# Routing and experts of layers 2 and 3 in one stage, with batched scores, a scan for the slot numbers and a table built from stationary one-hots

## The chip, the cores and the metric

The kernel runs on one core of one Trainium2 chip. The metric is the device time of one launch in microseconds (us). The engines are TensorE (PE: matmuls, and its weight loads, PEld), VectorE (DVE), ScalarE (ACT), GpSimd (POOL) and SyncE (SP, which here issues most DMA transfers). They run their own instruction streams and meet only at semaphores. L1666 is line 1666 of the kernel's source; `x4` behind a row is a count.

## The reference

A decoder of four layers works on x, 16 sequences of 112 tokens of 256 numbers, all in 32-bit floating point. Each layer adds a gated cross-attention and then a gated feed-forward part. In layers 2 and 3 the latter is a mixture of experts, of which each token uses its best two:

```python
# layer 2: 8 experts with 1024 hidden units, biases, RMS norm
xn = x * rsqrt(mean(x * x) + eps) * ln_w
vals, idx = top_k(xn @ Wg + bg, 2)
w = softmax(vals)
out = sum over the two experts e of w_e * ((silu(xn @ W1a[e] + b1a[e]) * (xn @ W1b[e] + b1b[e])) @ W2[e] + b2[e])
# layer 3: 9 experts with 704 hidden units
s, idx = top_k(sigmoid(x @ gate.T + bias), 2)
s = s / (sum(s) + 1e-20)
out = sum over the two experts e of s_e * ((silu(x @ w1[e].T) * (x @ w3[e].T)) @ w2[e].T)
# both: x = x + tanh(g_ffn) * out, where the part's own input is layernorm(x)
```

## The kernel before

The program is a list of stages in `flamingo`: attention and feed-forward for each layer. A stage is one `nc.Block()`, with one function for each engine, and all engines meet at its end. In layers 2 and 3 the feed-forward part is two such stages, `route_stage` and `experts_stage`.

`route_stage` (L1568) has 16 blocks of 112 tokens, with tokens on the partitions. DVE gathers mean and variance from `row_stats` (L164), POOL takes the root as a power (L109; in layer 2 twice, since the RMS factor follows from the first), and DVE writes the normed rows `r_kept` (L1832). SP stores each block to `p_rows` in device memory (L1666). For each block PE transposes two pieces (L1698), ACT copies them to `r_xT` (L1773, L1776), PE multiplies them, as stationary operand, with the gate weights (L1707) and adds the bias with a matmul of ones (L1714), and DVE copies 8 or 9 logits (L1845).

After all 16 blocks DVE finds the best two of each token (L1870, L1891) and writes them as one-hots, `r_chosen` (L1896). Each chosen pair of token and expert gets a slot; slots are numbered by expert, and each expert's slots are rounded up to whole tiles of 128. To number them, PE sums the one-hots over the tokens above and over all tokens (L1746), DVE sums over the 32 columns by doubling (L1922, L1923), turns the totals into tiles per expert and the expert of each tile, `p_expert` (L1940), and then into a slot per pair (L1942 to L1951). Then it writes which tile (`r_in_tile`, L1953 to L1958, once with the token's number and once with its share) and which place in the tile (`r_at_slot`, L1961) each pair has. PE multiplies the two (L1752, 32 matmuls with the 128 places as stationary operand and 70 or 72 columns): its result, the table, holds for each place and tile the token and its share. DVE turns it into `p_take`, `p_put` and `p_part` (L1967 to L1970). The stage ends.

`experts_stage` (L2070) runs over T tiles of 128 slots, 35 in layer 2 and 36 in layer 3. SP reads a tile's expert and loads that expert's weights (L2177, L2183, L2188), two tiles ahead: 1 MB each for w1, w3 and w2 in layer 2, some 2.2 MB in all in layer 3. POOL gathers the tile's rows (`e_x_in`, L2149), PE transposes them (L2215), ACT copies them to `e_xT` (L2257, L2260). PE then makes the hidden units chunk by chunk (L2226), ACT and DVE apply silu and product (L2270, L2297, L2302), PE multiplies with w2 (L2237), DVE scales (L2311, L2315), and POOL adds the rows to `p_sums` (L2160), which ACT's queue has filled with x at the stage's start (L2281). SP loads x back from the sums at the end (L2202).

Constants and weights of a later stage are noted with `core.request` and issued by SP where a stage calls `core.load_requested` (L119): in `experts_stage` behind tile 1, for the attention of layer 3. The attention weights lie in `attention_room`, those of layer 1's experts in `net_room`. The order on each engine is the order of the code.

## Time and profile before

| | |
|---|---|
| median of 3 runs | 2956.69 us (2954.8 to 2957.62) |
| profiled execution, its own time | 2955.2 us |
| its span, first to last instruction | 2953.2 us |
| granted TensorE clock, mean over the span | 0.942 |
| PE, PEld, DVE, ACT, POOL busy | 92%, 70%, 52%, 44%, 21% |
| routing and first expert matmul, layer 2 | 1735.08 to 1822.49 |
| routing and first expert matmul, layer 3 | 2561.90 to 2646.02 |

The time in the table's second line lies 2.0 us above the span, which is what is around it. A row of the timeline gives start and duration in us, engine, line, operation, tiles, count, and in brackets how long the engine was idle before and what it waited for. In the table of stretches the busy times stand in the order PE, PEld, DVE, ACT, POOL, with the number of rows, and the clock is a share of full speed, 1.00 for 2.4 GHz and 0.50 for 1.2 GHz. A 32-bit matmul leaves two rows, a transpose one.

### The profile page before, as it was taken

What the parts mean: (1) busy time and instruction counts of PE and PEld (TensorE: products, weight loads), DVE (VectorE), ACT (ScalarE), POOL (GpSimd) and SP (SyncE); (2) the same over time, 40 slices, a digit from 0 to 9 for tenths busy, and PEclk for the clock granted to TensorE, in tenths of its full rate; (3) what the DMA queues carried; (4) which work ended last, traced back from release to release, by engine and by line L of the source; (5) the groups of instructions that cost most, each with busy time, mean ns of one, the idle gap of its engine ahead of it and who ended that gap; (6) DMA issues with size and microseconds to landing.
All of it is one profiled execution on the core that took longest, in us unless ns stands there. A gap on an engine that the chain in (4) does not pass through costs nothing. (4 is left out here: it accounts for less than half of the span.)

```text
span 2953.2 us, 57870 instructions
## 1 busy us (share of the span) xinstructions
PE 2705.3 (92%) x20048; PEld 2068.7 (70%) x20048; DVE 1546.3 (52%) x4193; ACT 1297.9 (44%) x3605; POOL 616.9 (21%) x562
## 2 busy tenths in 40 slices
PE   6999978999999999698999975999988999859998
PEld 4777755666666666555666665999986777648887
DVE  4776666555555555345777743333326777532222
ACT  4777732433434434212766641333336777402222
POOL 1656550000000000001444410222220000003332
PEclk9999989999999999589999976999999999759999
DMA  3000010000000000010000005999971000039897
GB/s 118 17 17 17 12 69 8 13 7 13 13 7 13 12 7 1 29 32 8 17 23 17 17 26 187 337 327 331 325 242 31 22 18 23 19 111 308 307 308 239
DMA packets 92438, 269.24 MB, mean 91 GB/s; under 512 B 25672, under 2 KB 51528, under 8 KB 77864
## 3 DMA queue, kind: packets, MB, share of 16 engines
q1 hardware_dynamic: 74984, 244.21, 23.9%
q0 software_dynamic: 13632, 18.62, 2.9%
q10 hardware_dynamic: 3616, 3.67, 0.4%
q8 instruction: 128, 2.10, 0.3%
q14 instruction: 78, 0.64, 0.1%
HBM read 249.82 MB, written 18.48 MB: 91 GB/s over the span
## 5 line engine op out<-in xcount | busy, mean ns | idle before, releaser
L755 PEld LDWEIGHTS a_full_ps<-ident,a_probs 112*125 112x125 f32 x2688 | 368.0, 190 | 130.1 <-issue 63.6
L2226 PEld LDWEIGHTS e_ab_ps<-e_xT,e_w 128*128 128x128 f32 x3824 | 439.1, 193 | 20.2 <-issue 12.2
L2226 PE MATMUL e_ab_ps<-e_xT,e_w 128*128 128x128 f32 x3824 | 446.6, 277 | 5.5 <-DMA e_w<-in_L2f_w 2.3
L755 PE MATMUL a_full_ps<-ident,a_probs 112*125 112x112 f32 x2688 | 418.3, 281 | 18.7 <-DVE a_pT L1111 5.8
L862 ACT ACTIVATE a_probs<-a_masked,a_negmax 112x375 f32<-112x375 f32 x512 | 305.5, 599 | 280.3 <-DVE a_negmax L1085 280.2
L1111 DVE COPY a_pT<-a_full_ps 125x448 f32<-125x448 f32 x448 | 276.5, 621 | 254.0 <-PE a_full_ps L755 250.8
L656 PE MATMUL a_full_ps<-attention_room 128*125 128x256 f32 (+1 forms) x960 | 330.1, 472 | 10.9 <-ACT a_qT L854 3.3
L648 PE MATMUL a_full_ps<-attention_room 128*128 128x375 f32 x896 | 324.1, 490 | 1.4 <-ACT a_q_raw L850 0.7
L1085 DVE CUSTOM_DVE_ANT_0 a_masked<-a_sc_ps,a_mask_add 112x375 f32<-112x375 f32 x512 | 249.7, 544 | 29.9 <-PE a_sc_ps L742 29.9
L773 PEld LDWEIGHTS a_o_ps<-a_pT,a_v 125*32 125x32 f32 (+1 forms) x5376 | 164.0, 118 | 134.8 <-issue 106.7
L862 ACT ACTIVATE a_probs<-a_sc_ps,a_negmax 112x375 f32<-112x375 f32 x384 | 216.6, 576 | 91.1 <-DVE a_negmax L1091 91.0
L742 PE MATMUL a_sc_ps<-a_kT,a_qT 32*112 32x375 f32 (+1 forms) x1792 | 241.9, 514 | 5.1 <-ACT a_probs L862 3.1
L2237 PE MATMUL e_y_ps<-e_w,e_hid 128*128 128x256 f32 x992 | 232.9, 383 | 0.0
L656 PEld LDWEIGHTS a_full_ps<-attention_room 128*125 128x125 f32 x960 | 166.5, 189 | 92.4 <-issue 65.7
L773 PE MATMUL a_o_ps<-a_pT,a_v 125*32 125x112 f32 (+1 forms) x5376 | 216.0, 265 | 14.4 <-DVE a_pT L1111 10.8
L1091 DVE TENSOR_REDUCE a_negmax<-a_sc_ps 112x2 f32<-112x750 f32 x192 | 171.3, 934 | 95.0 <-PE a_sc_ps L742 95.0
L2160 POOL DMA_INDIRECT p_sums<-e_y_out,p_put x71 | 112.6, 1586 | 486.1 <-DVE e_y_out L2311 288.4
L648 PEld LDWEIGHTS a_full_ps<-attention_room 128*128 128x128 f32 x896 | 160.4, 194 | 71.3 <-issue 4.0
L2270 ACT ACTIVATE e_silu<-e_ab_ps,e_b 128x128 f32<-128x128 f32 x280 | 102.3, 367 | 242.4 <-PE e_ab_ps L2226 223.8
L2237 PEld LDWEIGHTS e_y_ps<-e_w,e_hid 128*128 128x128 f32 x992 | 179.9, 190 | 32.0 <-issue 11.9
L525 POOL TENSOR_TENSOR a_rstd<-a_rstd,minus_half 112x1 f32<-112x1 f32 x64 | 35.1, 549 | 781.4 <-DVE a_rstd L1008 774.3
L2297 DVE SCALAR_TENSOR_TENSOR e_hid<-e_ab_ps,e_b,e_silu 128x128 f32<-128x128 f32 x280 | 97.8, 351 | 172.1 <-ACT e_silu L2270 135.4
(251 smaller groups left out, 3629.3 us busy)
## 6 DMA issues: line engine op xcount, KB each, us to landing
e_w<-in_L2f_w SPq DMA_DIRECT2D x105, 1024.0 KB, 6.7
e_w<-in_L3f_w SPq DMA_DIRECT2D x72, 768.0 KB, 5.5
attention_room<-in_ctxT SPq DMA_DIRECT2D x64, 375.0 KB, 3.1
e_w<-in_L3f_w SPq DMA_DIRECT2D x36, 640.0 KB
e_b<-in_L2f_b SPq DMA_DIRECT2D x35, 128.0 KB, 7.8
p_rows<-r_kept SPq DMA_DIRECT2D x32, 112.0 KB, 1.8
p_sums<-x_all ACTq DMA_DIRECT2D x2, 1792.0 KB, 18.3
attention_room<-in_L0x_spline_wT SPq DMA_DIRECT2D x1, 2048.0 KB, 10.4
```

The source lines that it names most:

```text
L648: mm = pe.matmul(use_ps[:, 0:SK], wk[:, c, u[1] * P:(u[1] + 1) * P], ctxT[:, par, c, :], start=(c == 0), stop=(c == DC - 1))
L656: mm = pe.matmul(use_ps[0:KT, 0:v_width], ctxT[:, par, c, k * KT:(k + 1) * KT], wv[:, c, part * v_width:(part + 1) * v_width], start=(c == ...
L742: pe.matmul(sc_ps[:, a, 0:SK], lhs, kT[r:r + k, par, c, :], start=True, stop=True)\
L755: mm = pe.transpose(full_ps[0:KT, bank_of["turn", i, k], (j % 4) * S:(j % 4 + 1) * S], probs[:, i % 2, a, t * KT:(t + 1) * KT], ident[0:S, ...
L773: mm = pe.matmul(o_ps[a % WIDE * VW:(a % WIDE + 1) * VW, block * S:(block + 1) * S], v[:, par, t, head(i, a), :], pT[:, i % 2, KC * a + t, :],
L862: act.activation(probs[:, i % 2, a, 0:SK], src, ACT.Exp, bias=negmax[:, m:m + 1], scale=-1.0 if mask else 1.0, accum_out=rowsum[:, par, n: ...
L1085: dve.tensor_tensor_reduce(out=masked[:, i % 2, a, :], in0=sc_ps[:, a, 0:SK], in1=bias, scale=-1.0, scalar=FLT_MAX, op0=ALU.add, op1=ALU.m ...
L1091: dve.tensor_reduce(negmax[:, m:m + 2], sc_ps[:, 2 * a:2 * a + 2, 0:SK], AX.X, ALU.max, negate=True).then_inc(s_max.sem, 1)
L1111: dve.tensor_copy(pT[:, i % 2, 4 * k:4 * (k + 1), :], full_ps[0:KT, bank_of["turn", i, k], 0:4 * S] .rearrange("p (j s) -> p j s", j=4)).t ...
L2160: pool.indirect_dma_start(plan.sums, bass.IndirectOffsetOnAxis(plan.put[:, t:t + 1], 0), y_out[:, t % 2, :], None, compute_op=ALU.add).the ...
L2226: mm = pe.matmul(ab_ps[:, (par * FC + f) % RING, i * SLOTS:(i + 1) * SLOTS], w[:, par, c, f * P:(f + 1) * P], xT[:, c, :], start=(c == 0), ...
L2237: mm = pe.matmul(y_ps[:, par, 0:D], hid[parts[f], f, :], w2[parts[f], par, f, :], start=(f == 0), stop=(f == FC - 1))
```

## The change

One function, `moe_stage`, takes the place of both stages. What it does otherwise:

- Norm: three parts of 2, 6 and 8 blocks, one power each; in layer 2 the RMS factor is worked into the same power.
- Scores: blocks go in pairs, four pairs in flight in four PSUM banks. ACT copies a pair (448 numbers a partition). The gate weights, padded to 32 columns, are the stationary operand; four pairs are scored into the four quarters of a bank. The result is copied, turned back with two transposes, and DVE adds the bias. Best two and one-hots are made for each half of 8 blocks. In layer 2 DVE scales the gate weights by `ln_w`.
- Slots: one scan numbers a token's pairs by expert; PE sums only its last column, 8 or 9 columns. A second scan takes the place of the product with `before`.
- The expert list is finished ahead of the shares; SP waits for it alone (`s_expert`) and then loads weights.
- One-hots: four groups of 8 columns. DVE writes `spots`, the token part and the places; POOL multiplies `spots` by the share. PE takes 99 or 100 columns as stationary operand and 128 places as moving columns, group by group, then two transposes turn the table's rows and shares.
- Rooms: `in_tile`, `spots` and `xT` lie in `attention_room`, `at_slot` in `net_room`. So the loads for attention in layer 3 move behind tile 34.
- POOL clears semaphores after the norm. ACT's copy of x to the sums is its first instruction. PE has no instruction in its waits for the one-hots and for the first rows.

PE in layer 2, from the last scores to the first expert matmul. Before (`r_table_ps` is the table, `e_x_ps` the first tile's rows, `e_ab_ps` its hidden units):

```order
L1707 MATMUL r_l_ps<-route_room,r_xT 112x8 x2
L1714 MATMUL r_l_ps<-route_room,ones 112x8
L1707 MATMUL r_l_ps<-route_room,r_xT 112x8 x2
L1714 MATMUL r_l_ps<-route_room,ones 112x8
L1746 MATMUL r_count_ps<-r_chosen,route_room 112x256
L1746 MATMUL r_count_ps<-r_chosen,r_every_one 112x256
L1752 MATMUL r_table_ps<-r_in_tile,r_at_slot 128x70 x32
L1659 UNCONDITIONAL_BRANCH
L2208 UNCONDITIONAL_BRANCH
L2215 MATMUL e_x_ps<-ident,e_x_in 128x128 x2
L2226 MATMUL e_ab_ps<-e_xT,e_w 128x128 x32
```

The change (all results are in `m_banks`; 32x224 are scores of four pairs, 99x128 is the table):

```order
L2294 MATMUL m_banks<-ident,m_kept 128x112 x20
L2303 MATMUL m_banks<-attention_room,route_room 32x224 x8
L2294 MATMUL m_banks<-ident,m_kept 128x112 x4
L2310 MATMUL m_banks<-ident,m_logitsT 112x128 x2
L2294 MATMUL m_banks<-ident,m_kept 128x112 x8
L2303 MATMUL m_banks<-attention_room,route_room 32x224 x8
L2310 MATMUL m_banks<-ident,m_logitsT 112x128 x2
L2330 MATMUL m_banks<-m_order,route_room 112x8
L2330 MATMUL m_banks<-m_order,m_every_one 112x8
L2337 MATMUL m_banks<-net_room,attention_room 99x128 x32
L2342 MATMUL m_banks<-ident,m_table 128x35 x2
L2350 MATMUL m_banks<-ident,m_x_in 128x128 x2
```

The scores come in two lots of eight, the count has 8 columns, the table 128, and no block ends between table and first tile.

DVE in layer 2, from the count to the number of tiles of each expert. Before:

```order
L1919 COPY r_total_a<-r_count_ps 112x256
L1922 COPY r_total_b<-r_total_a 112x8
L1923 TENSOR_TENSOR r_total_b<-r_total_a 112x248
L1922 COPY r_total_a<-r_total_b 112x16
L1923 TENSOR_TENSOR r_total_a<-r_total_b 112x240
L1922 COPY r_total_b<-r_total_a 112x32
L1923 TENSOR_TENSOR r_total_b<-r_total_a 112x224
L1922 COPY r_total_a<-r_total_b 112x64
L1923 TENSOR_TENSOR r_total_a<-r_total_b 112x192
L1922 COPY r_total_b<-r_total_a 112x128
L1923 TENSOR_TENSOR r_total_b<-r_total_a 112x128
L1927 TENSOR_TENSOR r_over<-r_total_b,route_room 112x112
```

The change, from the scan (L2529) to the slot (L2552):

```order
L2529 SCALAR_TENSOR_TENSOR m_order<-m_again,m_chosen 112x256
L2533 TENSOR_TENSOR m_share<-m_best 112x16
L2541 TENSOR_TENSOR m_over<-m_banks,route_room 112x112
L2543 TENSOR_REDUCE m_tiles_of<-m_over 112x8
L2544 SCALAR_TENSOR_TENSOR m_ends<-m_every_one,m_tiles_of 112x8
L2545 TENSOR_TENSOR m_first<-m_ends,m_tiles_of 112x8
L2546 SCALAR_TENSOR_TENSOR m_first<-m_first,m_banks 112x8
L2550 TENSOR_TENSOR m_order<-m_order,m_first 112x256
L2551 TENSOR_TENSOR m_order<-m_order,m_chosen 112x256
L2552 TENSOR_REDUCE m_slot_f<-m_order 112x32
```

The scan stands ahead of the count, and the ten rows of doubling are gone.

SP in layer 2, from storing the normed rows to the first weights. Before:

```order
L1666 DMA p_rows<-r_kept 112x256 x16
L1659 UNCONDITIONAL_BRANCH
L2171 UNCONDITIONAL_BRANCH
L2174 DMA e_ln_w<-in_L2f_ln_w 128x2
L2177 TENSOR_LOAD p_expert
L2177 ISA x2
L2183 ISA
L2183 DMA e_w<-in_L2f_w 128x2048 x2
```

The change:

```order
L2250 DMA p_rows<-m_kept 112x2x256 x8
L2254 TENSOR_LOAD m_expert
L2254 ISA x2
L2260 ISA
L2260 DMA m_w<-in_L2f_w 128x2048 x2
```

A block end and a small load go; the expert is read, after a wait for the list, in the same stage in which the rows are stored.

```diff
+        plan = Plan(core, sb, layer, E)
+
+        lent = core.attention_room.lend()
+        in_tile, spots = lent([S, C, SHARES + T]), lent([S, C, T])
+        xT = lent([P, PAIRS, DC, 2 * S])
+        at_slot = core.net_room.lend()([S, C, P])
+        kept = sb("kept", [S, B, D])
+        logitsT, logits = sb("logitsT", [P, 2, 2 * S]), sb("logits", [S, B, E])
+        best, share, total = sb("best", [S, B, 8]), sb("share", [S, 2, B]), sb("total", [S, B])
...
+        banks = ps("banks", [P, 8, 512])
+        x_ps, lT_ps, l_ps = banks[:, 0:4], banks[:, 4:6], banks[0:S, 6:8]
+        count_ps, table_ps = banks[0:S, 4], banks[0:SHARES + T, 5]
+        rows_ps, shares_ps = banks[:, 6, 0:T], banks[:, 4, 0:T]
+        ab_ps, y_ps, in_ps = banks[:, 0:4], banks[:, 4:6], banks[:, 7]
+
+        norm_x = Norm(core, sb, sig, (2, 6, 8))
+        mv, rstd = norm_x.mv, norm_x.rstd
...
             @block.gpsimd
             def _(pool):
+                norm_x.on_gpsimd(pool)
+
+                pool.memset(in_tile[:, :, T:SHARES], 0.0).then_inc(s_zero.sem, 1)
                 core.clear_spent(pool)
+                for p in range(C // SPOTS):
+                    c = slice(p * SPOTS, (p + 1) * SPOTS)
+                    pool.wait_ge(s_in_tile.sem, p + 1)
+                    pool.tensor_tensor(in_tile[:, c, SHARES:], spots[:, c],
+                                       share[:].rearrange("s k b -> s (k b)")[:, c].unsqueeze(2)
+                                       .to_broadcast([S, SPOTS, T]), ALU.mult).then_inc(s_shares.sem, 1)

...
+                pool.wait_ge(s_take.sem, 1)
                 gather(0)
                 gather(1)
                 for t in range(T):
@@ -2170,8 +2245,10 @@

             @block.sync
             def _(sp):
-                if biased:
-                    sp.dma_start(ln_w[:], dram[name("ln_w")]).then_inc(s_ln.sem, 16)
+                for p in range(PAIRS):
+                    sp.wait_ge(s_xn.sem, 2 * p + 2)
+                    sp.dma_start(plan.rows[2 * p * S:2 * (p + 1) * S, :].rearrange("(b s) d -> s b d", s=S),
+                                 kept[:, 2 * p:2 * p + 2, :]).then_inc(s_kept.sem, 16)
...
+                    if isinstance(t, int) and t == 2 * ((T - 1) // 2):
                         core.load_requested(sp)

+                sp.wait_ge(s_expert.sem, 1)
                 each_tile(sp, body)
                 sp.wait_ge(s_put.sem, 16 * T)
...
+                def turn_pair(p):
+                    pe.wait_ge(s_xn.sem, 2 * p + 2)
+                    if p >= 4:
+                        pe.wait_ge(s_xT.sem, p - 3)
+                    for c in range(DC):
+                        for i in range(2):
+                            mm = pe.transpose(x_ps[:, p % 4, (2 * c + i) * S:(2 * c + i + 1) * S],
+                                              kept[:, 2 * p + i, c * P:(c + 1) * P], ident[0:S, 0:S])
+                    mm.then_inc(s_xps.sem, 1)
+
+                def score(h):
+
+                    pe.wait_ge(s_xT.sem, 4 * h + 4)
+                    for c in range(DC):
+                        for g in range(4):
+                            mm = pe.matmul(lT_ps[QUADRANT * g:QUADRANT * (g + 1), h, 0:2 * S], wg[:, c, :],
+                                           xT[:, 4 * h + g, c, :], start=(c == 0), stop=(c == DC - 1))
+                    mm.then_inc(s_lT.sem, 1)
+
+                def turn_score(h):
+                    pe.wait_ge(s_lTc.sem, h + 1)
+                    for i in range(2):
+                        mm = pe.transpose(l_ps[:, h, i * P:(i + 1) * P], logitsT[:, h, i * S:(i + 1) * S], ident[:])
+                    mm.then_inc(s_l.sem, 1)
+
+                pe.wait_ge(s_w.sem, 16 * len(loads))
+                if biased:
+                    pe.wait_ge(s_gate.sem, DC)
+                for p in range(4):
+                    turn_pair(p)
+                turn_pair(4)
+                score(0)
+                turn_pair(5)
+                turn_score(0)
+                turn_pair(6)
+                turn_pair(7)
+                score(1)
+                turn_score(1)
+
+                pe.wait_ge(s_order.sem, 1)
+                pe.wait_ge(s_zero.sem, 1)
+                for i, w in enumerate((below, every_one)):
+                    mm = pe.matmul(count_ps[:, i * E:(i + 1) * E], w[:], order[:, :, C - 1], start=True, stop=True)
+                mm.then_inc(s_count.sem, 1)
+
+                for c in range(C):
+                    if c % SPOTS == 0:
+                        pe.wait_ge(s_shares.sem, c // SPOTS + 1)
+                        pe.wait_ge(s_spots.sem, c // SPOTS + 1)
+                    mm = pe.matmul(table_ps[:, 0:P], in_tile[:, c, :], at_slot[:, c, :],
+                                   start=(c == 0), stop=(c == C - 1))
+                mm.then_inc(s_table.sem, 1)
+                pe.wait_ge(s_tablec.sem, 1)
+                for begin, turned in ((0, rows_ps), (SHARES, shares_ps)):
+                    mm = pe.transpose(turned, table[begin:begin + T, :], ident[begin:begin + T, begin:begin + T])
+                mm.then_inc(s_turned.sem, 1)
+
                 def turn(t, par):
...
+                def apply(k):
+                    dve.wait_ge(norm_x.ready, k + 1)
+                    part = norm_x.parts[k]
+                    for b in range(part.start, part.stop):
+                        dve.tensor_scalar(kept[:, b, :], x_all[:, b, :], mv[:, b, 0:1], rstd[:, b, :],
+                                          ALU.subtract, ALU.mult).then_inc(s_xn.sem, 1)
...
+                apply(0)
+                apply(1)
+                apply(2)
+                take_logits(0)
+                find_best(0)
+                choose(0)
+                take_logits(1)
+                find_best(1)
+                choose(1)
+
+                flat = lambda t: t[:].rearrange("s e c -> s (e c)")
+                done(dve.tensor_tensor_scan(flat(order), flat(again), flat(chosen), 0.0, ALU.mult, ALU.add))
+                dve.sem_inc(s_order.sem, 1)
+                if layer == 2:
+
+                    done(dve.tensor_tensor(share[:, 1, :], best[:, :, 1], best[:, :, 0], ALU.subtract))
+                    dve.sem_inc(s_to_act.sem, 1)
+                else:
+                    done(dve.tensor_tensor(total[:], best[:, :, 0], best[:, :, 1], ALU.add))
+                    done(dve.tensor_scalar(total[:], total[:], 1e-20, None, ALU.add))
+
+                dve.wait_ge(s_count.sem, 1)
+                earlier, in_all = count_ps[:, 0:E], count_ps[:, E:2 * E]
+                done(dve.tensor_tensor(over[:], in_all.unsqueeze(2).to_broadcast([S, E, LIMITS]),
+                                       limits[:].unsqueeze(1).to_broadcast([S, E, LIMITS]), ALU.is_gt))
+                done(dve.tensor_reduce(tiles_of[:], over[:], AX.X, ALU.add))
+                done(dve.tensor_tensor_scan(ends[:], every_one[:, 0:E], tiles_of[:], 0.0, ALU.mult, ALU.add))
+                done(dve.tensor_tensor(first[:], ends[:], tiles_of[:], ALU.subtract))
+                done(dve.scalar_tensor_tensor(out=first[:], in0=first[:], scalar=float(SLOTS), in1=earlier,
+                                              op0=ALU.mult, op1=ALU.add))
+
+
+                done(dve.tensor_tensor(order[:], order[:], first[:].unsqueeze(2).to_broadcast([S, E, C]), ALU.add))
+                done(dve.tensor_tensor(order[:], order[:], chosen[:], ALU.mult))
+                done(dve.tensor_reduce(slot_f[:], order[:].rearrange("s e c -> s c e"), AX.X, ALU.add))
...
+
+                done(dve.tensor_tensor(passed[:], tile_no[:].unsqueeze(2).to_broadcast([1, T, E]),
+                                       ends[0:1].unsqueeze(1).to_broadcast([1, T, E]), ALU.is_ge))
+                done(dve.tensor_reduce(expert_f[:], passed[:], AX.X, ALU.add))
+                done(dve.tensor_scalar(plan.expert[:], expert_f[:], float(E - 1), None, ALU.min))
+                dve.sem_inc(s_expert.sem, 1)
...
+                done(dve.tensor_scalar(share[:], share[:], gate, None, ALU.mult))
+
+                for p in range(C // SPOTS):
+                    c = slice(p * SPOTS, (p + 1) * SPOTS)
+                    b = slice(p * SPOTS % B, p * SPOTS % B + SPOTS)
+                    done(dve.tensor_tensor(spots[:, c], first_no[:].unsqueeze(1).to_broadcast([S, SPOTS, T]),
+                                           high[:, c].unsqueeze(2).to_broadcast([S, SPOTS, T]), ALU.is_equal))
+                    dve.sem_inc(s_in_tile.sem, 1)
+                    dve.tensor_tensor(in_tile[:, c, 0:T], spots[:, c],
+                                      token[:, b].unsqueeze(2).to_broadcast([S, SPOTS, T]), ALU.mult)
+                    dve.tensor_tensor(at_slot[:, c], slot_no[:].unsqueeze(1).to_broadcast([S, SPOTS, P]),
+                                      low[:, c].unsqueeze(2).to_broadcast([S, SPOTS, P]), ALU.is_equal)\
+                        .then_inc(s_spots.sem, 1)
+                dve.wait_ge(s_table.sem, 1)
+                dve.tensor_copy(table[:], table_ps[:, 0:P]).then_inc(s_tablec.sem, 1)
+                dve.wait_ge(s_turned.sem, 1)
+                dve.tensor_scalar(plan.take[:], rows_ps, 1.0, 0.0, ALU.subtract, ALU.max).then_inc(s_take.sem, 1)
+                done(dve.tensor_scalar(unused[:], rows_ps, 0.0, spare[:, 0:1], ALU.is_equal, ALU.mult))
+                dve.scalar_tensor_tensor(out=plan.put[:], in0=rows_ps, scalar=-1.0, in1=unused[:],
```

## Rows read from the trace of the kernel before

**Rows 1.** Busy time by stretch: us, busy us by engine, PE clock, DMA share, GB/s.
```profile
1792.00:1807.00 15.00, 13.93 (x64) 13.73 (x64) 4.28 (x8) 0.00 (x0) 0.00 (x0) 0.50 0.00 1
1807.00:1819.00 12.00, 0.00 (x0) 0.00 (x0) 0.00 (x0) 0.00 (x0) 2.19 (x2) 0.50 0.88 287
1823.00:1826.00 3.00, 3.00 (x19) 3.00 (x18) 0.00 (x0) 1.28 (x1) 0.00 (x0) 0.60 1.04 351
1826.00:1831.00 5.00, 5.00 (x47) 5.00 (x46) 2.09 (x7) 2.35 (x7) 0.00 (x0) 1.00 1.01 424
1880.00:2200.00 320.00, 320.00 (x2436) 308.00 (x2435) 97.91 (x268) 113.82 (x325) 75.34 (x58) 1.00 0.95 320
2646.00:2650.00 4.00, 3.98 (x18) 3.98 (x19) 0.29 (x1) 0.44 (x2) 0.00 (x0) 0.50 1.02 425
```

**Rows 2.** Timeline, start of layer 2's routing: start, us, engine, line, operation, count.
```profile
1735.08 0.15 DVE L1797 MEMSET r_every_one<- 112x112 f32 x1 [0.74 <-PEq L489]
...
1744.05 1.06 DVE L1832 TENSOR_SCALAR r_kept<-x_all,r_mv,r_rms 112x256 f32<-112x256 f32 x3
...
1744.61 0.98 PE L1698 MATMUL r_x_ps<-ident,r_kept 112*128 112x112 f32 x4 [11.36 <-DVE r_kept L1832]
```

**Rows 3.** Timeline, layer 2: choice, one pass, one-hots, table.
```profile
1771.40 1.19 DVE L1870 MAX8 r_best<-r_logits 112x8 f32<-112x8 f32 x16
...
1774.93 0.23 DVE L1893 CAST r_place<-r_at 112x128 f32<-112x128 uint32 x1
...
1783.61 0.42 DVE L1942 TENSOR_TENSOR r_total_a<-r_total_b,r_count_ps 112x256 f32<-112x256 f32 x1
...
1786.97 1.32 DVE L1953 TENSOR_TENSOR r_in_tile<-route_room,r_high 112x1120 f32<-112x1120 f32 x1
...
1791.00 4.63 DVE L1961 TENSOR_TENSOR r_at_slot<-route_room,r_low 112x1024 f32<-112x1024 f32 x4
...
1792.28 13.93 PE L1752 MATMUL r_table_ps<-r_in_tile,r_at_slot 112*128 112x70 f32 x64 [14.44 <-DVE r_at_slot L1961]
```

**Rows 4.** Timeline of layer 2's first tile; then gather L2149, issue to landing.
```profile
1808.91 2.19 SPq L2183 DMA_DIRECT2D e_w<-in_L2f_w  x2
1810.11 1.22 POOL L2149 DMA_INDIRECT e_x_in<-p_rows,p_take  x1 [66.30 <-issue]
...
1819.65 0.69 PE L2215 MATMUL e_x_ps<-ident,e_x_in 128*128 128x128 f32 x2 [13.45 <-DMA e_x_in<-p_rows,p_take]
...
1822.49 8.79 PE L2226 MATMUL e_ab_ps<-e_xT,e_w 128*128 128x128 f32 x64 [2.15 <-DMA e_w<-in_L2f_w]
```
```profile
DMA to landing us min/median/max: 3.2/6.2/9.9
```

**Rows 5.** Timeline, layer 3: stage start, sigmoid's table load, first expert matmul.
```profile
2561.90 0.15 DVE L1797 MEMSET r_every_one<- 112x112 f32 x1 [0.38 <-PEq L489]
...
2592.25 1.28 ACT L1786 ACT_TABLE_LOAD   x1
...
2646.02 7.75 PE L2226 MATMUL e_ab_ps<-e_xT,e_w 128*128 128x128 f32 x44 [1.84 <-DMA e_w<-in_L3f_w]
```

**Rows 6.** GpSimd's groups by shape; then its product of 256 elements, min/median/max.
```profile
L109 POOL TENSOR_TENSOR f_rstd<-f_rstd,minus_half 112x2 f32<-112x2 f32 x1 | 0.7, 710 | 12.6 <-issue 12.6
```
```profile
L531 POOL TENSOR_TENSOR x_all<-x_all,attention_room x48: 636/724/730, 476.0 to 2522.6; 112x256 f32<-112x256 f32 x48
```

**Rows 7.** Timeline: 12 matmuls with 32 x 112 results, at full clock.
```profile
2556.46 1.35 PE L773 MATMUL a_o_ps<-a_pT,a_v 125*32 125x112 f32 x24 [0.30 <-DVE a_pT L1111]
```

**Rows 8.** Timeline of SyncE's queue: moved loads end; last tile's load; x back.
```profile
1822.66 0.44 SPq L122 DMA_DIRECT2D attention_room<-in_L3x_bq  x1
...
1833.17 0.91 SPq L122 DMA_DIRECT2D attention_room<-in_ctxT  x2
...
2185.67 0.33 SPq L2190 DMA_DIRECT2D e_b<-in_L2f_b  x1
...
2209.12 7.38 SPq L2202 DMA_DIRECT2D x_all<-p_sums  x16
```

225 lines of the change are left out of this document (176 added, 49 removed).

## The prediction

> **What bounds the kernel now.** Read first the busy time by stretches [rows 1]. In the loop over expert tiles of layer 2 TensorE (PE) is busy 320.00 of 320.00 us at a granted clock of 1.00, with the DMA engines at 0.95: that loop is bound by PE, and the change leaves its instructions as they are. Ahead of each loop lies a head in which one engine after another works alone. While the table is made (1792 to 1807) PE is busy 13.93 us at 0.50 and DVE 4.28; from 1807 to 1819 PE does nothing and DMA stands at 0.88. Then read the timeline for how long the heads are. In layer 2 the first DVE row is at 1735.08 [rows 2] and the first expert matmul at 1822.49 [rows 4]: 87.4 us. In layer 3 they are at 2561.90 and 2646.02 [rows 5]: 84.1 us. All of it is on the path that sets the end. I therefore lay out the new head from its first DVE row (time 0) to its first expert matmul.
>
> **The change part by part, layer 2.**
>
> *Norm.* Before, the first kept row comes 9.0 us in (1744.05 against 1735.08, rows 2), behind two power operations of GpSimd (POOL) over 16 blocks. Now there is one, in parts of 2, 6 and 8, and the rms factor is folded into it. A part of 2 takes 0.71 us [rows 6]. DVE still needs its 16 aggregates (about 1.1), three memsets, two gate scalings and the waits between; I take 3.0 us to the first kept row. The second and third powers (about 1.3 and 1.7, between 0.71 for 2 and about 0.16 for each further block, an estimate) end under the rows that DVE is writing.
>
> *Turning and scoring.* Sixteen rows at 0.33 to 0.35 (1.06 for three, rows 2) end at 8.3. PE turns 32 pieces; four took 0.98 at half clock [rows 2], so 32 take 7.8, and it stays just behind DVE. The old loop interlocked each of 16 blocks with its copy by ScalarE (ACT); now four pairs are in flight. Score matmuls with 32 x 224 results have no row in the trace. Bounds: 24 rows (12 matmuls) of 32 x 112 took 1.35 us at full clock [rows 7], hence 0.11 each, 0.45 for twice the columns at half clock, 3.6 for eight. That count holds a fixed tail; run side by side on four column groups they could be 1.5. One behind the other, they would be 6. I take 3.0, nearer to the row. With copies, turn-back and waits I get logits of the first half at 13.2 and of the second at 20.0.
>
> *Best two and numbering.* MAX8 with its index search took 3.5 us for 16 blocks (1771.40 to 1774.93, rows 3). Now half of it lies under the second score; the other half ends at 21.8, the choice at 22.4. One scan replaces five doubling steps of a copy and a sum, with a subtraction and an addition behind them. The scan has no row: a DVE pass over 256 elements took 0.42 [rows 3], twice that is the upper bound, I take 0.5. The count on PE has 8 columns in place of 256: 0.7 with its waits. After that come five small operations (0.2 to 0.3 each, by the cast of 0.23), three of 256 elements (0.45 with the gap), four of 32 (0.22) and three for the list of experts (two of 280 at 0.47, one small): the list stands at 28.3, the shares at 29.2.
>
> *Weights.* SyncE (SP) starts them there; before, at 1808.91 [rows 4], 73.8 us in. Both first tiles are some 6.5 MB, at the rates of [rows 1] (287 to 424 GB/s) 15 to 23 us, so they land at 44 to 51 after 28.3. This takes the wait for weights off the path, or nearly, and lets the first row gather run into their tail. The copy of x to the sums, which before ran beside these loads, starts at time 0 and has 28 us to itself.
>
> *One-hots and table.* Four groups of DVE work in place of one block: 0.37 + 0.37 + 1.16 each (a quarter of 1.32, about a quarter of 1.40 and of 4.63, rows 3), so ends at 31.2, 33.1, 35.1 and 37.0. POOL multiplies by the shares beside it. PE runs 32 matmuls of 128 columns as each group comes. Before, 32 took 13.93 us at half clock, 0.435 each, bound by their weight loads [rows 3]; that would end at 45.2. But what moves now is 128 columns, not 70. In the trace 70 columns left the clock at 0.50 for 13.93 us of work; expert matmuls, 128 columns and a full row, were at 0.60 on average one to three us after they began and at 1.00 from 1826 on; in layer 3 the first 4 us are still at 0.50 [rows 1]. I take the nearer likeness: ten table matmuls at half clock (4.4) and 22 at 0.235 (5.2), the table done at 41.0.
>
> *To the first expert matmul.* Copy of the table, two transposes and the rows to take: 1.4. The old gap between the table's last matmul (1792.28 + 13.93 = 1806.21, rows 3) and the gather (1810.11) held a block boundary and POOL's clearing of semaphores; now 0.3. The gather took 9.5 us to PE's first transpose, 1810.11 to 1819.65 [rows 4]; over the kernel it is 3.2 at least, 6.2 in the median, 9.9 at most. The loads are nearly out; I take 5.0. Transposes and copy, 1.6. The first expert matmul is at 49.3: 38.1 us earlier.
>
> **Layer 3.** The same with 9 experts and 36 tiles (0.4 more), no gate scaling (0.35 less), and two sigmoids of which the second, with its round trip, is on the path (0.7; the 1.28 us table load [rows 5] runs ahead of its wait, under the score). Only 4.4 MB of weights are ahead of the gather, so it lands after 3.5. First expert matmul at 48.9, against 84.1: 35.2 us earlier.
>
> **Costed at nothing.** Loads for attention in layer 3 move from behind tile 1 to behind tile 34. SP issued its last weight load at 2185.67 and its next transfer, x back from the sums, at 2209.12; the issues that move took 11.4 us (1822.66 to 1834.08) under full DMA load [rows 8]. So 23 us cover them. Without that cover they would cost up to those 11.4 us. Tile 0 still starts at half clock, as before: PE idles between table and rows in both.
>
> **Sum.** 38.1 + 35.2 = 73.3 us. The profiled execution took 2955.2 us (span 2953.2), the median of the runs is 2956.69. 2956.7 - 73.3 gives **2883 us**.
>
> **The rivals.** *The table stays at half clock.* Its matmuls have 112 rows and come in bursts, which speaks for it; the table of before, equally busy at 0.50, too. Price 4.2 us a layer, of which the gather returns about 0.8 in layer 2: 2883 + 7.6 = 2891 us. The Trainium skill, "TensorE: Matmul & The Clock Gate", The HAM clock gate, says that activity releases the half clock and idleness brings it back; by that alone the old table's 13.93 us of work should have been released too, and the trace shows that it was not.
>
> *DVE and POOL get in each other's way.* POOL's share product has two SBUF inputs, like DVE's one-hots beside it. In this trace a POOL product of 256 elements is 0.64 to 0.73 us [rows 6], whatever runs beside it, so if each of four waits for the other the groups end at up to 39.8 in place of 37.0, the last eight matmuls end 1.9 later, at 41.7, and the first group is 0.7 late as well. That is 1.4 us a layer at most, 2.8 in all: 2886 us. The Trainium skill, "SBUF — State Buffer", Who interferes with whom, holds that the pair of ports that both share is locked for a whole instruction and that a DVE instruction with two SBUF inputs contends with a GpSimd one that reads SBUF; no row here shows them apart.
>
> *The gather runs into the weights.* If it takes 9.5 us in both layers as before, 4.5 + 6.0 are lost: 2894 us. For it: DMA at 0.88 to 1.01 while tile weights load. Against: before, the x copy and two tiles' weights had all begun within 3 us of it; now they have 13 us of start.
>
> *Slower than before.* The loops become bound by DMA. The 71 tiles would have to take 1.04 us more each (73.3 / 71), in layer 2 on top of 10.8 (82 rows a tile, 2436 rows in 320 us, rows 1), which is when a tile's transfers need 10% more DMA time than now, share 0.95 to over 1.04. It would come if the gathers and the sums' additions landed so late in every tile that PE waited for them. At 1.2 us a tile it gives 2883 + 85 = 2968 us. Against it: order, sizes and rings of the loop stay as they are.
>
> *It doesn't do what it says.* If the parts do not overlap (a wait for all of s_w or for the zeroing stands late), the head shrinks by the removed work alone, some 20 us a layer: 2917 us. Against it: the gate weights are asked for a whole attention stage earlier.
>
> **How the numbers follow.** Forecast 0.50; half clock 0.22; DVE and POOL 0.12; gather 0.11; no overlap 0.03; slower 0.02. The range has to take in the score bounds (-1.5 to +3 for each of four, of which I allow -6 and +6 in all), the gather (-1.8 to +10.5) and the half clock (+7.6), not all at once: **2868 to 2903 us**. A change of 0.2% (5.9 us) is about what a measurement can tell from none: faster 0.97, within 0.2% 0.01, slower 0.02.
>
> **What would show it.** Right: the head of layer 2, from first DVE row to first expert matmul, at 46 to 53 us and layer 3 within 2 us of it; weights on SP about 28 us in; PE's granted clock above 0.5 in the last third of the table; tiles at 10.8 us as before. Wrong: score groups over 4 us each, a gather over 8 us, DVE groups over 2.5 us apart, PE waiting for weights in the loop, or attention in layer 3 waiting for its own.

## The result, and the profile of the changed kernel

The changed kernel takes 2877.15 us (median of 4 runs, 2873.78 to 2878.14), the kernel before beside it 2957.15 us (4 runs, 2954.8 to 2960.83): a ratio of 0.9726, 95% interval 0.971 to 0.9743. Run again later, with the combined version below, it took 2876.51 us (5 runs, 2872.05 to 2879.04). The forecast was 2883 us with a range of 2868 to 2903; the time is 5.9 us under the forecast and inside the range. The profiled execution has a span of 2876.3 us, 1.8 us under its own time of 2878.1, at a mean granted clock of 0.958.

The stretches of the changed kernel that answer to [rows 1]: first the making of layer 2's table, the time until its first rows have landed, its first tile, then its loop, then layer 3's table. Columns as there (us, busy us of PE, PEld, DVE, ACT, POOL with row counts, clock, DMA share, GB/s):

```profile
1767.90:1772.00 4.10, 4.10 (x19) 4.10 (x20) 3.81 (x6) 0.00 (x0) 1.31 (x2) 0.50 1.00 420
1772.00:1775.40 3.40, 3.40 (x30) 3.19 (x29) 3.25 (x4) 0.00 (x0) 0.65 (x1) 0.98 0.92 274
1778.00:1785.70 7.70, 0.24 (x2) 0.12 (x2) 0.55 (x3) 0.20 (x1) 2.20 (x2) 0.78 0.90 364
1789.00:1792.00 3.00, 3.00 (x16) 3.00 (x16) 0.61 (x2) 2.00 (x3) 0.00 (x0) 0.50 0.02 3
1850.00:2150.00 300.00, 300.00 (x2272) 288.45 (x2272) 91.00 (x249) 106.34 (x305) 71.07 (x55) 1.00 0.98 329
2558.00:2564.00 6.00, 5.12 (x44) 4.59 (x42) 3.71 (x5) 0.00 (x0) 0.67 (x1) 1.00 0.92 376
```

The loop is as it was: PE busy 300.00 of 300 us at full clock. The table was made at half clock for its first 4.1 us and at full clock after that.

The timeline of the changed kernel in layer 2 from the first DVE row to the second tile, answering to [rows 2 to 4] (`attention_room` holds `in_tile` and `spots`, `net_room` holds `at_slot`):

```profile
1739.72 0.25 DVE L2467 BATCH_NORM_AGGREGATE m_mv<-row_stats 112x2 f32<-112x6 f32 x2 [0.67 <-PEq L496]
1742.40 6.00 DVE L2487 TENSOR_SCALAR m_kept<-x_all,m_mv,m_rstd 112x256 f32<-112x256 f32 x16
...
1747.65 1.72 PE L2303 MATMUL m_banks<-attention_room,route_room 128*32 128x224 f32 x16
...
1752.65 0.96 PE L2303 MATMUL m_banks<-attention_room,route_room 128*32 128x224 f32 x16 [0.63 <-ACT attention_room L2391]
...
1757.41 0.69 DVE L2529 TENSOR_TENSOR_SCAN m_order<-m_again,m_chosen 112x256 f32<-112x256 f32 x1
...
1763.73 0.17 DVE L2561 TENSOR_SCALAR m_expert<-m_expert_f 1x35 int32<-1x35 f32 x1
...
1764.95 0.84 SPq L2260 DMA_DIRECT2D m_w<-in_L2f_w  x2
1765.03 0.45 DVE L2578 TENSOR_TENSOR attention_room<-route_room,m_high 112x280 f32<-112x280 f32 x1
1765.62 0.65 POOL L2214 TENSOR_TENSOR attention_room<-attention_room,m_share 112x280 f32<-112x280 f32 x1 [20.92 <-DVEq L2580]
1765.63 0.95 DVE L2581 TENSOR_TENSOR attention_room<-attention_room,route_room 112x280 f32<-112x280 f32 x1
...
1766.51 1.21 DVE L2583 TENSOR_TENSOR net_room<-route_room,m_low 112x1024 f32<-112x1024 f32 x1
...
1767.87 7.54 PE L2337 MATMUL m_banks<-net_room,attention_room 112*99 112x128 f32 x48 [8.73 <-DVE net_room L2583]
...
1775.64 1.96 PE L2337 MATMUL m_banks<-net_room,attention_room 112*99 112x128 f32 x16 [0.24 <-DVE net_room L2583]
1777.64 0.29 DVE L2587 COPY m_table<-m_banks 99x128 f32<-99x128 f32 x1 [2.15 <-PE m_banks L2337]
...
1779.36 1.24 POOL L2221 DMA_INDIRECT m_x_in<-p_rows,m_take  x1 [5.31 <-DVE m_take L2589]
...
1785.75 0.69 PE L2350 MATMUL m_banks<-ident,m_x_in 128*128 128x128 f32 x2 [7.51 <-DMA m_x_in<-p_rows,m_take]
...
1787.31 9.91 PE L2361 MATMUL m_banks<-m_x_inT,m_w 128*128 128x128 f32 x64 [0.87 <-ACT m_x_inT L2425]
...
1800.73 1.50 PE L2361 MATMUL m_banks<-m_x_inT,m_w 128*128 128x128 f32 x12
```

Counted from the first row, each at its start: kept rows +2.7, expert list +24.0, weights +25.2, the table's copy +37.9, gather +39.6, first expert matmul +47.6. Before it was +87.4, so this head is 39.8 us shorter.

Layer 3 in the changed kernel, answering to [rows 5]:

```profile
2524.45 0.25 DVE L2467 BATCH_NORM_AGGREGATE m_mv<-row_stats 112x2 f32<-112x6 f32 x2 [0.33 <-PEq L496]
...
2563.82 0.29 DVE L2587 COPY m_table<-m_banks 100x128 f32<-100x128 f32 x1 [2.15 <-PE m_banks L2337]
...
2565.50 1.10 POOL L2221 DMA_INDIRECT m_x_in<-p_rows,m_take  x1 [5.27 <-DVE m_take L2589]
...
2568.39 0.69 PE L2350 MATMUL m_banks<-ident,m_x_in 128*128 128x128 f32 x2 [3.97 <-DMA m_x_in<-p_rows,m_take]
...
2569.64 7.35 PE L2361 MATMUL m_banks<-m_x_inT,m_w 128*128 128x128 f32 x44 [0.57 <-ACT m_x_inT L2428]
```

The first expert matmul is at +45.2, where it was at +84.1: 38.9 us shorter.

SyncE's queue at the end of layer 2's loop, with the loads that moved, answering to [rows 8]:

```profile
2149.96 0.56 SPq L122 DMA_DIRECT2D attention_room<-in_L3x_bq  x1
...
2155.10 0.91 SPq L122 DMA_DIRECT2D attention_room<-in_ctxT  x2
2173.08 7.37 SPq L2280 DMA_DIRECT2D x_all<-p_sums  x16
```

They are issued within 6.1 us and 17 us ahead of SP's next transfer. They cost nothing, as the sum below shows.

The spans add up: 2953.2 before; the stretch ahead of layer 2's routing came out 4.6 us longer (1739.72 against 1735.08; attention and earlier layers, which the change does not touch); the heads gave 39.8 and 38.9; from layer 2's first expert matmul to layer 3's first row it is 2.3 us less (739.41 before, 737.14 after, by the rows at 1822.49 and 2561.90 of before); the last 0.5 us is behind it: 2953.2 + 4.6 - 39.8 - 38.9 - 2.3 - 0.5 = 2876.3.

From tile 1 to layer 3's first row alone it is 3.4 us less (727.1 and 723.7). About 1.5 us of this can be put down to the loads that moved. In the kernel before, PE waited twice at tile 2, 0.18 us for weights and 1.32 us for the first hidden units, and these for that tile's biases, which were queued behind the attention loads:

```profile
1851.12 3.84 PE L2226 MATMUL e_ab_ps<-e_xT,e_w 128*128 128x128 f32 x32 [1.32 <-DVE e_hid L2297]
```

In the changed kernel PE has no wait in layer 2 from tile 1 on, and neither has the version below whose weights start late. The move was not tested by itself, and the rest of the 3.4 us is open.

The 4.6 us is variation: in the eleven other profiled executions of versions of the new stage, the same place lay at 1734.8 to 1740.1 us with nothing altered ahead of it.

### The profile page after: what moved, and what is told of

Its sections match the earlier page's. It is cut to its first block and busy times, and to the rows that moved or that the text cites. A ratio compares the mean times of both kernels' runs of the same rounds, so it can differ in the third digit from the quotient of the medians.

```text
span 2876.3 us, 57313 instructions
## 1 busy us (share of the span) xinstructions
PE 2664.5 (93%) x19932; PEld 2026.4 (70%) x19932; DVE 1534.6 (53%) x4152; ACT 1293.8 (45%) x3580; POOL 623.3 (22%) x575
## 5 line engine op out<-in xcount | busy, mean ns | idle before, releaser
L2361 PEld LDWEIGHTS m_banks<-m_x_inT,m_w 128*128 128x128 f32 x3824 | 439.8, 194 | 15.5 <-issue 13.8
L2361 PE MATMUL m_banks<-m_x_inT,m_w 128*128 128x128 f32 x3824 | 447.0, 278 | 1.4 <-ACT m_x_inT L2425 0.9
L663 PE MATMUL a_full_ps<-attention_room 128*125 128x256 f32 (+1 forms) x960 | 330.2, 472 | 10.7 <-ACT a_qT L861 3.1
L2372 PE MATMUL m_banks<-m_w,m_hid 128*128 128x256 f32 x992 | 232.9, 383 | 0.0
L2233 POOL DMA_INDIRECT p_sums<-m_y_out,m_put x71 | 112.6, 1586 | 482.4 <-DVE m_y_out L2617 286.4
L2439 ACT ACTIVATE m_silu<-m_banks,m_b 128x128 f32<-128x128 f32 x280 | 102.8, 367 | 241.0 <-PE m_banks L2361 229.5
L2372 PEld LDWEIGHTS m_banks<-m_w,m_hid 128*128 128x128 f32 x992 | 179.9, 190 | 32.0 <-issue 11.9
L2603 DVE SCALAR_TENSOR_TENSOR m_hid<-m_banks,m_b,m_silu 128x128 f32<-128x128 f32 x280 | 98.1, 351 | 163.8 <-ACT m_silu L2439 163.8
```

The source lines that it names most:

```text
L663: mm = pe.matmul(use_ps[0:KT, 0:v_width], ctxT[:, par, c, k * KT:(k + 1) * KT], wv[:, c, part * v_width:(part + 1) * v_width], start=(c == ...
L2233: pool.indirect_dma_start(plan.sums, bass.IndirectOffsetOnAxis(plan.put[:, t:t + 1], 0), y_out[:, t % 2, :], None, compute_op=ALU.add).the ...
L2361: mm = pe.matmul(ab_ps[:, (par * FC + f) % RING, i * SLOTS:(i + 1) * SLOTS], w[:, par, c, f * P:(f + 1) * P], x_inT[:, c, :], start=(c == ...
L2372: mm = pe.matmul(y_ps[:, par, 0:D], hid[parts[f], f, :], w2[parts[f], par, f, :], start=(f == 0), stop=(f == FC - 1))
```

## The experiments

Unless said otherwise a version is the changed kernel with one edit. "Head" is the stretch from the first statistics row (DVE) to the first expert matmul, and a number with a plus is us from that row. The theory to be tested: in the changed kernel DVE's groups bound the table, weights in flight the landing of layer 2's first rows, and PE's clock the first tile. The rival for the table is PE at half clock, for the rows the gather's own latency, and for the first tile its weights. "Tile 1" is PE's first up-projection matmul of the second tile, in the changed kernel at +61.0 in layer 2 and +55.5 in layer 3. Since a run wanders by up to 5 us ahead of the head, small differences are read in the head and not in the medians alone. The versions ran on several chips, beside each the kernel before, whose medians there were 2957.0 to 2959.8 us; the ratios are to that kernel.

**Who slows DVE in the one-hots?** In the changed kernel the product L2581 takes 0.95 us for 280 elements, its neighbour L2578 of the same size 0.45. The edit moves the share product from POOL to ACT, as 32 copies with a scale:

```diff
-                    pool.tensor_tensor(in_tile[:, c, SHARES:], spots[:, c],
...
+                for c in range(C):
+                    if c % SPOTS == 0:
+                        act.wait_ge(s_in_tile.sem, c // SPOTS + 1)
+                    ins = act.activation(in_tile[:, c, SHARES:], spots[:, c, :], ACT.Copy,
+                                         scale=flat_share[:, c:c + 1])
+                    if c % SPOTS == SPOTS - 1:
+                        ins.then_inc(s_shares.sem, 1)
```

> The product of the one-hots with the shares moves from GpSimd to ScalarE (32 copies with a scale, 35 or 36 elements each). Theory 'DVE and POOL get in each other's way' (in the changed kernel the DVE product beside POOL's takes 0.95 us, its twin L2578 alone 0.44): the DVE product falls to about 0.45, a group of one-hots from 2.61 to 2.1 us, the last group ends 2.0 us earlier in each layer, some 4 us in all: 2873 us. Rival 'the 0.95 us is the strided output, not POOL': the DVE product stays at 0.95, the time stays at 2877 us, or rises if 32 ScalarE copies (over 0.2 us each, 6.4 us) end later than DVE's groups.

Measured: 2873.62 us (2871.66 to 2873.97), ratio 0.9715 (0.9699 to 0.9731). Its timeline in layer 2:

```profile
1762.31 1.83 ACT L2415 ACTIVATE attention_room<-attention_room,m_share 112x35 f32<-112x35 f32 x8 [6.83 <-DVEq L2582]
1762.37 0.45 DVE L2583 TENSOR_TENSOR attention_room<-attention_room,route_room 112x280 f32<-112x280 f32 x1
...
1764.19 10.26 PE L2331 MATMUL m_banks<-net_room,attention_room 112*99 112x128 f32 x64 [8.33 <-ACT attention_room L2415]
```

The product is back at 0.45 and groups start 2.09 us apart instead of 2.59. In layer 3 the time from the expert list to the copied table falls from 13.85 to 12.95 us. In layer 2 it does not fall (14.02 against 13.91): PE's 64 rows are now one piece of 10.26 us, at a clock that stays at 0.50 until about 1770, so with DVE out of the way the half clock is what bounds the table. The list itself was 1.2 us earlier in this run (+22.8); that is no effect of the edit, since the unaltered kernel, run again, shows it at +22.7 too (below). So the time is the one expected, but not for the reason given: of the 2 us a layer expected at the table layer 2 shows nothing and layer 3 0.9 us.

Is it any write by POOL, or its reads? The second edit has POOL write zeros instead of the product:

```diff
-                    pool.tensor_tensor(in_tile[:, c, SHARES:], spots[:, c],
-                                       share[:].rearrange("s k b -> s (k b)")[:, c].unsqueeze(2)
-                                       .to_broadcast([S, SPOTS, T]), ALU.mult).then_inc(s_shares.sem, 1)
+                    pool.memset(in_tile[:, c, SHARES:], 0.0).then_inc(s_shares.sem, 1)
```

> GpSimd writes zeros in place of the share product, with the same waits and signals; the shares are thereby left out of the result (every expert's part is multiplied by 0), all other work stays. Theory 'the shared read path': DVE's product beside it falls from 0.95 to about 0.45, as in the run with the shares on ScalarE, since GpSimd now reads nothing: 2873 us. Rival 'any GpSimd write in SBUF holds DVE up': it stays near 0.9 and the time at 2877 us.

Measured: 2874.9 us (2869.34 to 2878.56), ratio 0.972 (0.9704 to 0.9736).

```profile
1760.97 0.34 POOL L2214 MEMSET attention_room<- 112x280 f32 x1 [20.84 <-DVEq L2578]
1761.01 0.45 DVE L2579 TENSOR_TENSOR attention_room<-attention_room,route_room 112x280 f32<-112x280 f32 x1
```

POOL works at the same moment and writes the same bytes, and DVE takes 0.45. So it is POOL's reading beside a DVE instruction with two SBUF inputs that costs DVE 0.50 us each time. The Trainium skill, "SBUF — State Buffer", Who interferes with whom, says this: such a DVE instruction contends with a GpSimd instruction that reads SBUF, and not with one that only writes it; the two traces agree.

**Fewer, larger groups.** Two groups of 16 instead of four of 8:

```diff
-SPOTS = 8
+SPOTS = 16
```

> One-hots in two groups of 16 columns in place of four of 8. Theory 'DVE's groups bound the table': DVE's total work stays (some 10.4 us less two starts), PE has 16 matmuls left after the last group in place of 8: 1.9 us more a layer at full clock, 3.5 if the clock has not risen since PE starts 2.5 us later: 2881 to 2884 us. Rival 'the table's matmuls are hidden wherever they stand': 2877 us.

Measured: 2878.54 us (2877.96 to 2879.16), ratio 0.9728 (0.9711 to 0.9744). From list to table 16.16 us in layer 2 (13.91) and 15.49 in layer 3 (13.85), so four groups are worth 2.2 and 1.6 us at the table. At tile 1 only 0.2 us of it is left in layer 2 (+61.2), where the gather, asked for later, took 4.7 us instead of 6.4: the rows of layer 2 wait for something that ends at its own time. In layer 3 0.6 us is left (+56.1), tile 0 having found its clock sooner (6.50 us instead of 7.35). The median is 1.4 us over the changed kernel's, which is within what one kernel moves by itself, and under the 2881 to 2884 us expected: the loss at the table is real, most of it does not reach tile 1.

**What do the first rows wait for?** In layer 2 the gather takes 6.4 us to PE's transposes (1779.36 to 1785.75), in layer 3 only 2.9. The edit lets SP ask for tile 1's weights in layer 2 only when the first rows have landed:

```diff
                 def body(t, par):
+                    if biased and isinstance(t, int) and t == 1:
+                        sp.wait_ge(s_x[0].sem, 16)
                     load(t, par)
```

> In layer 2 SyncE holds back the loads of tile 1 until the first rows have landed. Theory 'the gather runs into the weights': it took 6.4 us to PE's first transpose in layer 2 (DMA share 0.97) and 2.9 us in layer 3, where the loads were done; it falls to about 3 in layer 2, 3.4 us less: 2874 us, and tile 1 still has its weights in time (10 us needed, 12 to 13 there). Rival 'the 6.4 us is the gather's own' : same time, or 2 to 5 us more if tile 1 now waits for weights.

Measured: 2870.78 us (2869.93 to 2872.14), ratio 0.9709 (0.9693 to 0.9726).

```profile
1774.66 1.24 POOL L2221 DMA_INDIRECT m_x_in<-p_rows,m_take  x1 [5.32 <-DVE m_take L2591]
...
1777.68 0.69 PE L2352 MATMUL m_banks<-ident,m_x_in 128*128 128x128 f32 x2 [4.15 <-DMA m_x_in<-p_rows,m_take]
...
1779.24 9.87 PE L2363 MATMUL m_banks<-m_x_inT,m_w 128*128 128x128 f32 x64 [0.87 <-ACT m_x_inT L2427]
```

and the stretch from the gather's issue to PE's transposes:

```profile
1774.60:1777.70 3.10, 0.02 (x1) 0.02 (x1) 0.00 (x0) 0.00 (x0) 2.20 (x2) 0.99 0.14 42
```

3.0 us with DMA at 0.14, as in layer 3 of the changed kernel (2.9 at 0.16), where it had been 6.4 us with DMA at 0.90; and tile 1 at +57.6 instead of +61.0. The rows had waited 3.4 us for tile 1's weights, which are not needed until a tile later. Held back they still arrived in time: PE went from tile 0 into tile 1 without a wait for them. The medians lie 6.4 us apart; the trace gives the edit 3.4 of them, and its head began 4.7 us earlier than the first trace's, with nothing altered ahead of it.

The opposite edit starts all weights only with the table:

```diff
-                sp.wait_ge(s_expert.sem, 1)
+                sp.wait_ge(s_take.sem, 1)
```

> SyncE waits for the rows to take, not for the experts' list, so the first weights start about 14 us later in each layer, at the time of the first gather, as in the kernel before. Theory 'the early weights are a term of the gain': 2 MB for the first product must land after that, 8 us or more with everything else in flight, so the first expert matmul comes 2 to 6 us later in each layer: 2882 to 2888 us. Rival 'the weights were hidden by the gather anyway, and early loads only slow the gather': under 1 us a layer lost or even gained, 2875 to 2879 us.

Measured: 2883.73 us (2880.78 to 2886.45), ratio 0.9744 (0.9727 to 0.976). In layer 2:

```profile
1779.70 0.84 SPq L2260 DMA_DIRECT2D m_w<-in_L2f_w  x2
...
1786.31 0.69 PE L2350 MATMUL m_banks<-ident,m_x_in 128*128 128x128 f32 x2 [7.83 <-DMA m_x_in<-p_rows,m_take]
1787.87 6.17 PE L2361 MATMUL m_banks<-m_x_inT,m_w 128*128 128x128 f32 x32 [0.87 <-DMA m_w<-in_L2f_w]
1793.09 1.28 ACT L2439 ACT_TABLE_LOAD   x1 [5.37 <-DMA m_b<-in_L2f_b]
1795.31 3.84 PE L2361 MATMUL m_banks<-m_x_inT,m_w 128*128 128x128 f32 x32 [1.27 <-DVE m_hid L2603]
```

Tile 1 starts at +62.7 in layer 2 (1.7 later) and at +59.1 in layer 3 (3.6 later, the gather now at 6.4 us there too). So the weights' early start is worth 5.3 us in all, which is also the difference of the ratios. It was expected at the first expert matmul, 2 to 6 us a layer. There it is 0.3 us in layer 2, where the rest lies in tile 0: PE waits 1.27 us for DVE, and DVE for ACT, which had waited for the late biases. In layer 3 it is 3.6 us, nearly all of it the gather, 6.4 us instead of 2.9. That it is no more is, I take it, because the late weights land while a gather of 6 us is under way.

**What does the cold clock cost the first tile?** Tile 0's 64 rows of up-projection take 9.91 us, in the loop 7.31; the clock of the changed kernel is 0.50 until about 1792.5. The edit gives PE 30 (layer 3: 14) matmuls of constants, results unused, ahead of its wait for the first rows:

```diff
+                for _ in range(30 if biased else 14):
+                    pe.matmul(banks[:, 0, 0:P], ident[:], ident[:], start=True, stop=True)
                 turn(0, 0)
```

> PE runs 30 (layer 2) or 14 (layer 3) matmuls of 128 columns into a free PSUM bank between the table's last transposes and the first rows. Theory 'the first tile pays for PE's idle wait': the clock is still at full speed when the rows come, tile 0's first product falls from 9.9 to 7.3 us in layer 2 and from 7.35 to 5.2 in layer 3: 4.8 us less, 2872 us. Rival 'tile 0 waits for something else' (weights of tile 0, the activation table of ScalarE, silu): under 1 us gained, 2876 us; if the fill outlasts the wait, up to 2 us lost.

Measured: 2869.97 us (2867.42 to 2873.47), ratio 0.9702 (0.9686 to 0.9718). Stretches and the first tile:

```profile
1775.00:1780.00 5.00, 4.62 (x42) 4.36 (x41) 0.84 (x4) 0.20 (x1) 2.20 (x2) 1.00 1.01 425
1785.30:1792.70 7.40, 7.36 (x66) 7.39 (x67) 2.27 (x7) 3.64 (x8) 0.39 (x1) 1.00 0.07 21
```
```profile
1785.34 7.38 PE L2361 MATMUL m_banks<-m_x_inT,m_w 128*128 128x128 f32 x64 [0.87 <-ACT m_x_inT L2427]
```

Tile 0 takes 7.38 us, and tile 1 begins at +58.6 (61.0) and +53.2 (55.5): 2.4 + 2.2 us.

The same with 27 more such matmuls ahead of the wait for the one-hots:

```diff
+                for _ in range(27):
+                    pe.matmul(banks[:, 0, 0:P], ident[:], ident[:], start=True, stop=True)
                 for c in range(C):
                     if c % SPOTS == 0:
                         pe.wait_ge(s_shares.sem, c // SPOTS + 1)
```

> As the run with the fill before the rows, and 27 more such matmuls in the wait between count and one-hots. Theory 'DVE's groups bound the table, not PE's clock': the table's first 24 matmuls run at full clock but PE waits for each group, the last 8 take 1.96 us as now, the end of the table stays: 2872 us, the same as with the first fill alone. Rival 'the half clock costs in the table': up to 3 us less in each layer, 2866 us.

Measured: 2870.35 us (2869.33 to 2872.89), ratio 0.9708 (0.9692 to 0.9725). The table is ready no sooner, 13.91 us behind the list as before, though each group of 16 rows now takes 1.96 us from the first on: PE waits 0.63 us for DVE in each group. With POOL's product beside DVE, DVE's groups bound the table and the clock does not.

**One norm part instead of three.**

```diff
-        norm_x = Norm(core, sb, sig, (2, 6, 8))
+        norm_x = Norm(core, sb, sig, (16,))
...
-                apply(1)
-                apply(2)
```

> The norm is one part of 16 blocks again (one power of 2.9 us). Theory 'the split takes POOL's power off the path': first kept row 2.2 us later in each layer and all behind it too: 4 us more, 2881 us. Rival 'PE and ACT behind it had slack' (they run at DVE's pace with waits): under 1 us a layer, 2878 us.

Measured: 2879.92 us (2875.93 to 2880.43), ratio 0.9728 (0.9712 to 0.9745). The first kept row moves from +2.7 to +4.4 in layer 2 and from +2.4 to +4.5 in layer 3. In layer 3 all of it arrives: list +27.7 against +25.5, tile 1 +57.8 against +55.5. In layer 2 nothing does: list +24.1, tile 1 +61.1. In that run PE's first eight scores took 0.96 us instead of 1.72, its clock having come up earlier. The split is worth 2.2 us in layer 3; in layer 2 it is hidden by the clock's variation, and what it is worth there stays open.

**All three together.** Shares on ACT, tile 1's weights behind the first rows, and 14 matmuls of constants ahead of the rows; and with it the changed kernel again, on the same chip.

> Three edits of the earlier runs together: the 32 share products on ACT instead of POOL (in both layers), tile 1's weight loads in layer 2 held back until the first rows have landed, and 14 filler matmuls on PE in both layers before it waits for the first rows. If the savings are independent: from the changed kernel's 2877 us, 4 us for the shares (0.9 + 1.2 us at the tables of the two layers and the expert list's earlier end in layer 2), 3.4 us for the gather of layer 2 (6.4 us down to 3.0), and 4.8 us for the first tiles on a clock that is already up (2.5 + 2.3 us), so 2864 to 2866 us. The rival: the last two were both measured at 6 to 7 us from the same 61.0 us at which tile 1 begins, and overlap there, because the first tile's up weights land as late as before and PE then waits for them; then 2869 to 2870 us. Which it is stands in the time from the first statistics row of layer 2 to tile 1's first matmul: about 54 us by the first, 57 to 58 us by the second.

> The changed kernel unaltered, on the same chip as the combined one, so that the two are compared side by side. Its time should be 2877 us, within 3 us; the start of layer 2's routing in it is expected anywhere in 1735 to 1740 us, since that place differed by so much between the profiled runs so far. If instead it begins at 1735 us here and the time is 5 us less than 2877 us, the variation in the start is a variation in the time.

Measured: the combined version 2864.64 us (5 runs, 2862.79 to 2869.91), ratio to before 0.9689 (0.9676 to 0.9702); the changed kernel beside it 2876.51 us, 0.9726 (0.9713 to 0.9739). The combined one is 11.9 us faster and the fastest of this study. Its layer 2, the first tiles:

```profile
1780.34 7.38 PE L2357 MATMUL m_banks<-m_x_inT,m_w 128*128 128x128 f32 x64 [0.87 <-ACT m_x_inT L2431]
...
1791.23 7.31 PE L2357 MATMUL m_banks<-m_x_inT,m_w 128*128 128x128 f32 x64
```

The head began at 1737.19, so tile 1 is at +54.0, where the first possibility was put (54; the other at 57 to 58), and at +51.8 in layer 3. Against the repeated run's +58.8 and +55.9 that is 8.8 us, against the first trace 10.7. The single edits had shown 3.4, 2.4 + 2.2 and, at layer 3's table, 0.9 us, together 8.9: the gains add. The table is now bound by PE again: it takes 9.48 us, of which the first part is at half clock. Matmuls of constants ahead of the one-hots, idle in the earlier version, might now take up to 2 us a layer more; that was not tried.

The repeated run also shows how far one kernel moves by itself. Its layer 2 had the list at +22.7 and tile 1 at +58.8, against +24.0 and +61.0. The list's part of it is seen in the first eight scores:

```profile
1744.59 1.29 PE L2303 MATMUL m_banks<-attention_room,route_room 128*32 128x224 f32 x16
```

They took 1.29 us, 1.72 in the first trace: the clock came up in the midst of them, and in the other run behind them. The head began at 1736.65 there, 3.1 us earlier than in the first trace, and the execution took 2872.05 us against 2878.1: about half of the 6 us lies ahead of the head, so the variation there is a variation of the time.

**Why did the clock rise in the new table and never in the old one?** In the kernel before, PE was busy for 13.93 us at 0.50 [rows 3]. First possibility: the columns moved, 70 of them. This is the kernel before with three blocks moved in place of two:

```diff
-                        mm = pe.matmul(table_ps[:, 0:2 * T], at_slot[:, c, :],
-                                       in_tile[:, c, 1:3, :].rearrange("s v t -> s (v t)"),
+                        mm = pe.matmul(table_ps[:, 0:3 * T], at_slot[:, c, :],
+                                       in_tile[:, c, 0:3, :].rearrange("s v t -> s (v t)"),
...
-                    rows_ps, part_ps = table_ps[:, 0:T], table_ps[:, T:2 * T]
+                    rows_ps, part_ps = table_ps[:, T:2 * T], table_ps[:, 2 * T:3 * T]
```

> The kernel before, with one thing altered: the two-column-block matmuls that add up the table in layers 2 and 3 move three blocks (105 columns) instead of two (70 columns), the third being sums that nothing reads. The question is what kept TensorE's granted clock at 0.50 over the 13.9 us of that table while PE was busy throughout. If the moved columns decide it, the clock rises above 0.50 within the table and the stretch takes less than 13.9 us although it does more; if not, it stays at 0.50, and 64 matmuls of 105 columns take as long as 64 of 70 (13.9 us, if the weight load sets their pace) or up to 1.5 times that, 20.9 us (if the columns do).

Measured: one run, 2956.57 us beside 2957.71. Row and stretch of layer 2's table:

```profile
1793.44 13.98 PE L1752 MATMUL r_table_ps<-r_in_tile,r_at_slot 112*128 112x105 f32 x64 [14.44 <-DVE r_at_slot L1961]
```
```profile
1793.50:1807.50 14.00, 13.92 (x64) 13.67 (x64) 3.33 (x4) 0.00 (x0) 0.00 (x0) 0.50 0.01 1
```

Half as many columns again, the same 13.98 us, the same 0.50, and in layer 3 too. PEld is busy for 13.67 of the 14 us: the weight loads set the pace, and the 35 extra columns are free and change nothing. As many as 128 were not moved here.

Second possibility: the roles. The change also made `in_tile` the stationary operand and `at_slot` the moving one. This is the combined version with the roles of before:

```diff
-                    mm = pe.matmul(table_ps[:, 0:P], in_tile[:, c, :], at_slot[:, c, :],
+                    mm = pe.matmul(table_ps[:, 0:SHARES + T], at_slot[:, c, :], in_tile[:, c, :],
...
-                pe.wait_ge(s_tablec.sem, 1)
-                for begin, turned in ((0, rows_ps), (SHARES, shares_ps)):
-                    mm = pe.transpose(turned, table[begin:begin + T, :], ident[begin:begin + T, begin:begin + T])
...
```

> The combined kernel with the operands of the table's matmuls exchanged back to the roles they had before the change: at_slot (128 columns) stationary, in_tile (99 columns) moving. The table then comes out with places on the partitions, so its copy and the two transposes fall away, and the ACT copy of the shares waits for DVE's put. Two questions. First the clock: in the kernel before, PE was busy for 13.9 us with at_slot stationary and the clock stayed at 0.50, with 70 or with 105 columns moving; in the combined kernel, with in_tile stationary and 128 columns moving, it rose about 4 us after the table began and the 64 rows took 9.48 us. If the roles decide it, the clock stays at 0.50 and the table takes about 13.9 us, 4.4 us more a layer: 2864.6 + 2 x (4.4 - 0.7) = 2872 us. If it is something else (the DMA transfers beside it, the scoring before it), the table takes 9.3 to 9.8 us, and the turn that falls away saves 0.6 to 0.7 us a layer: 2863.3 us, with the gather of layer 2 asked for at +38.1 instead of +38.8 us from the first statistics row.

Measured: 2872.13 us (5 runs, 2870.41 to 2880.35), ratio 0.9722 (0.9709 to 0.9735), which is 7.5 us slower than the combined version (on another chip, where the kernel before took 2957.66 us, beside the combined one 2957.71). Table and stretch in layer 2, the version with the roles of before first, then the combined one:

```profile
1762.36 13.98 PE L2333 MATMUL m_banks<-attention_room,net_room 112*128 112x99 f32 x64 [8.34 <-ACT attention_room L2415]
```
```profile
1762.40:1776.30 13.90, 13.90 (x65) 13.90 (x66) 5.56 (x9) 5.48 (x24) 0.00 (x0) 0.50 0.52 209
```
```profile
1764.73 9.48 PE L2333 MATMUL m_banks<-net_room,attention_room 112*99 112x128 f32 x64 [8.34 <-ACT attention_room L2419]
```
```profile
1764.70:1774.20 9.50, 9.46 (x64) 9.27 (x64) 5.63 (x9) 5.48 (x24) 0.00 (x0) 0.75 0.76 309
```

Everything ahead of the table is the same, the scores and the DMA transfers too, and PE is busy all the time in both. With the old roles the clock stays at 0.50 for 13.98 us, with the new ones it rises and the table takes 9.48. In layer 3 it is 13.98 against 8.98. So the exchange of operands is what lifts the clock, worth 4.5 and 5.0 us of table less about 0.6 each for the two turns; at tile 1 it is 3.8 and 4.7 us (+57.9 and +56.5 against +54.0 and +51.8).

What in the exchange does it is in part open. A stationary operand of 128 columns does not by itself hold the clock at 0.50. The version with both fills has such matmuls ahead of the table in layer 2, 128x128 stationary and 128 columns moving:

```profile
1754.55 7.65 PE L2334 MATMUL m_banks<-ident 128*128 128x128 f32 x54
```

They begin at 0.50 and the clock is 1.00 from 1758 on. But they fill 128 rows, the table's matmuls 112, so whether it is the 128 columns moving instead of 99, or something else that differs, no run here tells apart.

## Why the prediction was right, point by point

- **What bounds the kernel.** Right. The heads gave 78.7 us, forecast 73.3, and the loop kept its 10.8 us a tile.
- **Norm, transposes, kept rows.** Right within 0.4 us: first kept row +2.7 (3.0), kept rows ended at +8.7 (8.3).
- **Scores.** Mis-sized, and the largest term that was: 1.72 and 0.96 us for eight matmuls (16 rows), taken as 3.0 each. The row [rows 7] was doubled for twice the columns and again for half clock, 0.45 us a matmul. But the 1.72 us were all at 0.50, 0.215 a matmul, and at full clock one took 0.12 us, hardly more than the 0.11 of a matmul with half the columns. So it is the doubling for the columns that failed, and the lower bound for matmuls side by side, 1.5, was the better one. The second half's logits came at +14.9, predicted 20.0; the steps from there to the list took 0.8 us more than forecast, and the list came at +24.0, predicted 28.3.
- **The scan.** 0.69 us, taken as 0.5, under its upper bound of 0.84.
- **One-hots.** The groups were 2.59 us apart, not 1.9, which is over the 2.5 us that the prediction itself had named as a sign of being wrong. The rival of DVE and POOL in each other's way did happen: 0.50 us on each of four products, 0.9 us at layer 3's table by the version without it, where the rival had said 1.4 a layer. (By its own working that should have been 0.7: a first group 0.7 late and a last group that puts the end at 41.7 instead of 41.0 are the same delay.) The forecast's own steps had left it out. The rest of the difference is 0.45 for passes taken as 0.37, and 1.21 for 1.16.
- **The clock in the table.** Right: 19 rows, two a matmul, in the 4.1 us at 0.50, where ten matmuls had been said; the rival of a table that stays at half clock did not come. The likeness chosen (expert matmuls with 128 columns moving) pointed the right way; why it did was not known. The price of 4.2 us a layer was near as well: the table took 9.7 and 9.8 us from its first matmul to its last, and 64 rows that stay at 0.50 took 13.98, so the rise gave an estimated 4.2 us. More was not to be had here: at full clock from the first row on, PE only waited for DVE's groups.
- **Table to gather.** 1.72 us from the copy's start to the gather, taken as 1.7.
- **Gather.** The wait was 6.4 us in layer 2, taken as 5.0 because "the loads are nearly out". They were not: tile 1's weights held the rows for 3.4 us. In layer 3 it was 2.9, taken as 3.5. The rival named the mechanism, but its 9.5 us in both layers did not come.
- **First expert matmul.** +47.6 and +45.2, predicted +49.3 and +48.9. Down layer 2's chain against the forecast: list 4.3 us early, the first group's start 3.9, last group's end 1.2 (the groups), table done 3.1 (PE had kept up, and only eight matmuls were left), rows landed 1.7, first expert matmul 1.7. In layer 3, with a gather shorter than forecast, 3.7 were left. Together 5.4, the difference between 78.7 and 73.3. Layer 3's 48.9 does not follow from its terms, which give 48.55 (49.3 + 0.4 - 0.35 + 0.7 - 1.5); the forecast would still round to 2883.
- **Loads for attention in layer 3.** Right that they cost nothing: 17 us of cover were left. That the traces would show some 1.5 us at tile 2 gained by the move was not foreseen.
- **First tile at half clock.** Said, and rightly, but not priced: 2.4 and 2.2 us over a tile at full clock. Before it cost something too (8.79 and 7.75 us, rows 4 and 5), so the sum suffered little: tile 1 came 38.7 and 39.3 us earlier, 0.7 us less in all than the first matmuls.
- **Slower, and no overlap.** Neither came: PE is busy for all of the 300 us of the loop, though the DMA share rose from 0.95 to 0.98.
- **Signs and range.** Layer 2's head, 47.6 us, lies in the 46 to 53 named, layer 3's 2.4 us from it and not within 2, and the weights started 25 us in and not 28. The range's lower end, 2868, lies 7 us below what its terms give (2883 - 6 - 1.8 = 2875).

The profiled executions differ by 77.1 us (2955.2 - 2878.1), the medians by 80.0: the late start of that one head, 4.6 us, covers the difference. That the sum came so near is partly luck, since the errors had both signs: scores too dear, groups and layer 2's gather too cheap.

## What to carry to other kernels

When a serial head is rebuilt, write down for each operation what else is reading or landing at the time: the two terms that came out too low were a DVE pass beside a GpSimd one that read SBUF, and rows queued behind weights that nobody needed yet. Where PE is busy but its weight loads set the pace, look at the granted clock of the stretch and try the operands the other way round; here that was worth about 4 us a layer, where starting the weights 14 us earlier was worth 2.7 a layer. And before an effect of 1 to 5 us is believed, look at the same kernel twice and at the milestones between two rows of one trace, since the start of this head wandered by 5 us.

## What the runs showed of the hardware

- PE busy without a gap for 13.93 to 13.98 us, two rows per matmul, with 112 x 128 stationary and 70, 99, 105 or 108 columns moving: granted clock 0.50 throughout. With 112 x 99 or 100 stationary and 128 columns moving it rose from 0.50 to 1.00 between 3.2 and 6.2 us into the table, in both layers of all ten traces in which it stood at 0.50 before. The Trainium skill, "TensorE: Matmul & The Clock Gate", The HAM clock gate, says that activity releases the half clock; by the busy time of these rows alone the two should have gone alike, and the traces show that they did not.
- With 128 x 128 stationary and 128 columns moving it rose from 0.50 too, about 3 us after the first such matmul (both fills, layer 2).
- Eight matmuls with 32 x 224 results in the four quarters of a bank took 1.72 us at 0.50 and 0.96 at 1.00.
- Moving 105 columns instead of 70 in a matmul of 32-bit data whose weights change each time cost nothing (13.98 us for 64 rows against 13.93).
- A GpSimd product that reads two SBUF inputs beside a DVE product of 280 elements a partition: 0.95 us instead of 0.45. A GpSimd memset of the same bytes: 0.45.
- An indirect gather of 128 rows reached PE in 3.0 us beside a DMA share of 0.14, and in 6.4 us beside 0.90 (layer 2 of the changed kernel) or 0.83 (layer 3 with late weights).
- A scan over 256 elements a partition took 0.69 us on DVE, where an ordinary pass took 0.42.
